# State space stage: squares of two chunks added on GpSimd, tail decays read off the decays, late decays moved beside the result, halves' bank moved

## The reference

```python
def ssd(x, A, B, C, chunk):
    ...
    Acs = jnp.cumsum(Ac, axis=-1)
    Lmat = jnp.exp(segsum(Ac))
    Y_diag = jnp.einsum('bclhn,bcshn,bhcls,bcshp->bclhp', Cc, Bc, Lmat, xc)
    decay_states = jnp.exp(Acs[..., -1:] - Acs)
    ...
    Y_off = jnp.einsum('bclhn,bchpn,bhcl->bclhp', Cc, states, jnp.exp(Acs))
    return (Y_diag + Y_off).reshape(b, l, h, p)

def mamba2_block(x, in_w, conv_w, conv_b, dt_bias, A_log, D, norm_w, out_w):
    ...
    zxbcdt = x @ in_w.T
    ...
    xBC = jax.nn.silu(y.transpose(0, 2, 1) + conv_b)
    dt = jax.nn.softplus(dt + dt_bias)
    ...
    y = ssd(xh * dt[..., None], A * dt, Bh, Ch, CHUNK)
    y = y + D[None, None, :, None] * xh
    ...
    y = rmsnorm(y * jax.nn.silu(z), norm_w)
    return y @ out_w.T
```

## Time and profile before

| | us |
|---|---|
| median of 3 runs | 2408.68 (2407.0 to 2409.1) |
| span of the profiled execution | 2405.4 |
| the state space stage in it | about 545 to 1022 |

### The profile page before, as it was taken

One profiled execution on the slowest core, in us unless ns is written; L12 is line 12 of the kernel. 1 busy time (PEld: TensorE's weight loads), 2 busy tenths in 40 slices (PEclk: granted clock), 3 DMA queues, 4 the chain that ended last, 5 costly groups with the idle time before them and its releaser, 6 DMA issues.

```text
span 2405.4 us, 39635 instructions
## 1 busy us (share of the span) xinstructions
PE 1979.7 (82%) x14320; PEld 1331.4 (55%) x14320; DVE 1549.6 (64%) x3583; ACT 1312.5 (55%) x2684; POOL 482.1 (20%) x539
## 2 busy tenths in 40 slices
PE   6999775988999999858874287999999898668796
PEld 4666562446777777633452154666666577424465
DVE  6877675766666666548849945766666456658543
ACT  4666533766777777525765235666666312337632
POOL 2112003204323323223004521001100001031033
PEclk9999986998999999968997588999999899869997
DMA  4000004400000000015301000000000100154012
GB/s 183 1 1 1 1 1 123 135 25 36 1 1 1 1 1 1 1 35 159 89 1 72 0 10 1 1 1 1 1 1 1 46 8 1 56 177 133 22 55 76
DMA packets 80162, 88.04 MB, mean 37 GB/s; under 512 B 6578, under 2 KB 70115, under 8 KB 78945
## 3 DMA queue, kind: packets, MB, share of 16 engines
q1 hardware_dynamic: 78625, 83.01, 11.1%
q0 software_dynamic: 1344, 2.49, 0.4%
HBM read 54.91 MB, written 30.70 MB: 36 GB/s over the span
## 4 chain that ended last, share of the span: by engine, by line
PE 56%; DVE 25%; ACT 8%; issue 7%; DMA 2%; POOL 1%; SPq 0%; DVEq 0%; ACTq 0%; POOLq 0%
PE bank L469 48%; DVE scratch L1226 3%; DVE w_keep L1927 2%; PE bank L653 1%; PE bank L2962 1%; PE bank L368 1%; DVE stats L245 1%; PE bank L693 1%; ACT w_early L3203 1%; DVE scratch L3101 1%; DVE scratch L721 1%; DVE w_early L2539 1%; DVE XN L3136 1%; PE bank L1195 1%; DVE scratch L3126 1%
## 5 line engine op out<-in xcount | busy, mean ns | idle before, releaser
L469 PE MATMUL bank<-scratch 64*128 64x256 bf16 (+5 forms) x3696 | 399.8, 320 | 81.9 <-DMA scratch<-parts 40.2
L469 PEld LDWEIGHTS bank<-scratch 64*128 64x128 bf16 (+3 forms) x3696 | 220.5, 123 | 231.7 <-issue 79.8
L1226 DVE TENSOR_REDUCE scratch<-bank 128x2 f32<-128x512 f32 x384 | 245.7, 686 | 97.5 <-PE bank L469 94.9
L469 PE MATMUL bank<-w_keep,scratch 128*128 128x128 f32 (+4 forms) x1760 | 247.1, 332 | 35.7 <-ACT scratch L806 20.8
L1312 ACT ACTIVATE w_keep<-bank 128x512 f32<-128x512 f32 x384 | 210.9, 597 | 70.0 <-PE bank L469 64.3
L469 PE MATMUL bank<-XNT,w_keep 128*128 128x256 f32 (+4 forms) x800 | 237.1, 435 | 7.2 <-POOL w_keep L2175 2.5
L469 PEld LDWEIGHTS bank<-w_keep,scratch 128*128 128x128 f32 (+3 forms) x1760 | 184.4, 185 | 97.2 <-issue 45.9
L3203 ACT ACTIVATE w_early<-bank,scratch 128x256 f32<-128x256 f32 x256 | 123.8, 564 | 130.9 <-DVE scratch L3105 130.9
L469 PEld LDWEIGHTS bank<-XNT,w_keep 128*128 128x128 f32 x800 | 148.7, 196 | 60.7 <-issue 29.4
L469 PE MATMUL bank<-w_early,scratch 64*128 64x256 f32 (+3 forms) x1152 | 164.9, 347 | 12.2 <-ACT w_early L3203 8.5
L469 PEld LDWEIGHTS bank<-w_early,scratch 64*128 64x128 f32 (+3 forms) x1152 | 119.7, 185 | 67.3 <-issue 41.3
(11 more groups left out here) (450 smaller groups left out, 3792.3 us busy)
## 6 DMA issues: line engine op xcount, KB each, us to landing
scratch<-parts SPq DMA_DIRECT2D x24, 1024.0 KB, 5.1
parts<-scratch SPq DMA_DIRECT2D x192, 96.0 KB, 2.4
parts<-scratch SPq DMA_DIRECT2D x96, 64.0 KB, 2.1
w_early<-pack_l3f SPq DMA_DIRECT2D x1, 5206.0 KB, 16.0
w_keep<-pack_l2f SPq DMA_DIRECT2D x1, 2124.0 KB, 13.7
w_early<-pack_mamba SPq DMA_DIRECT2D x1, 2120.0 KB, 19.0
w_keep<-pack_l2x SPq DMA_DIRECT2D x1, 2049.0 KB, 9.0
w_keep<-taps SPq DMA_DIRECT2D x4, 512.0 KB, 5.5
```

Source lines behind the costliest of these rows:

```text
L469: return pe.matmul(out, lhsT, rhs, start=start, stop=stop, skip_group_check=True)
L1226: dve.tensor_reduce(neg[:, :, h], self.k.bank[5 - g % 2][:, :].rearrange("p (t s) -> p t s", s=S), AXX, ALU.max, negate=True).then_inc(*s. ...
```

## The change

Four edits, all in `StateSpace`:

1. GpSimd gets a new instruction for each unit, `squares_pool(n-3)`, last in its iteration: it adds the squares of the two chunks in place. `mean_pe` then needs two matmuls where there were four, and waits for this sum (`s.pool.at("sq", ...)`) where it waited for ScalarE's squares.
2. The tail decays are no longer made by a matmul: ScalarE reads the last column of each head from the decays' bank in a 128x4 instruction of its own (in `decay_act`, t = 0), and `late_act` shrinks from 260 to 256 columns.
3. `late_pe` moves from the start of iteration u+1 into iteration u, behind the second part of the convolution and ahead of `result_pe`. Its use of bank 2 now comes after the output of unit n-5.
4. The `off` product moves from bank 2 to bank 0, which it shares with `raw` (`raw_bank`).

```diff
@@ -1690,7 +1690,13 @@
     def late_bank(self, n):
 
         s, there = self.k.s, lambda u: 0 <= u < UNITS
-        uses = [("late", n - 1, s.weighed, "late"), ("root", n - 5, s.lowered, "root"), ("out", n - 5, s.added, "final"), ("off", n - 2, s.normed, "off")]
+        uses = [("root", n - 5, s.lowered, "root"), ("out", n - 5, s.added, "final"), ("late", n, s.weighed, "late")]
+        return [x for x in uses if there(x[1])]
+
+    def raw_bank(self, n):
+
+        s, there = self.k.s, lambda u: 0 <= u < UNITS
+        uses = [("raw", n, s.stacked, "raw"), ("off", n - 2, s.normed, "off")]
         return [x for x in uses if there(x[1])]
 
     def small_bank(self, n):
@@ -1728,8 +1734,7 @@
     def raw_pe(self, pe, u):
         s, b, bank = self.k.s, u % B, self.k.bank[0]
         self.entered(pe, u)
-        if u >= 1:
-            pe.wait_ge(*s.stacked.at("raw", u - 1))
+        self.freed(pe, self.raw_bank, u, "raw")
         for j in range(2):
             m = mm(pe, bank[:, j * S:(j + 1) * S], self.weight(u, "xbc")[:, (INNER + j) * P:(INNER + j + 1) * P], self.k.XNT[:, b * S:(b + 1) * S])
         m.then_inc(*s.projected.up("raw", u))
@@ -1762,11 +1767,11 @@
         bank = self.k.bank[2]
         if u % PAIR == 0:
             pe.wait_ge(*s.formed.at("a", u))
-        self.freed(pe, self.late_bank, u + 1, "late")
+        self.freed(pe, self.late_bank, u, "late")
         for h in range(H_SSM):
             rows, cols = slice(HP * (h % 2), HP * (h % 2 + 1)), slice(h // 2 * P, (h // 2 + 1) * P)
-            mm(pe, bank[rows, cols], a3[:, 1, h:h + 1].to_broadcast([P, HP]), self.upto)
-        mm(pe, bank[:, S:S + H_SSM], self.k.w["after"], a3[:, 0, :]).then_inc(*s.scored.up("late", u))
+            m = mm(pe, bank[rows, cols], a3[:, 1, h:h + 1].to_broadcast([P, HP]), self.upto)
+        m.then_inc(*s.scored.up("late", u))
 
     def decay_pe(self, pe, u, t):
         s = self.k.s
@@ -1797,7 +1802,7 @@
         m.then_inc(*s.turned.up("x", u))
 
     def result_pe(self, pe, u):
-        s, out, late, xd, wt = self.k.s, self.k.bank[7], self.k.bank[2], self.xd[u % 2], self.by_head(self.wt[u % 2])
+        s, out, off, xd, wt = self.k.s, self.k.bank[7], self.k.bank[0], self.xd[u % 2], self.by_head(self.wt[u % 2])
         pe.wait_ge(*s.formed.at("xd", u))
         pe.wait_ge(*s.divided.at("weights", u))
         pe.wait_ge(*s.pool.at("weights", u))
@@ -1809,24 +1814,23 @@
                 m = mm(pe, out[rows, cols:cols + P], xd[:, t * D_INNER + h * HP:t * D_INNER + (h + 1) * HP], wt[:, t, h, :])
         m.then_inc(*s.summed.up("y", u))
         pe.wait_ge(*s.pool.at("xu", u))
-        self.freed(pe, self.late_bank, u + 2, "off")
+        self.freed(pe, self.raw_bank, u + 2, "off")
         for c in range(INNER):
-            m = mm(pe, late[:, c * P:(c + 1) * P], self.xu[u % 2][:, c * P:(c + 1) * P], self.gm[u % 2][:, 2 * P:3 * P])
+            m = mm(pe, off[:, c * P:(c + 1) * P], self.xu[u % 2][:, c * P:(c + 1) * P], self.gm[u % 2][:, 2 * P:3 * P])
         m.then_inc(*s.summed.up("off", u))
 
     def mean_pe(self, pe, u, j):
 
 
         s, bank = self.k.s, self.k.bank[3]
-        pe.wait_ge(*s.flip_s.at("sq", u + j))
+        pe.wait_ge(*s.pool.at("sq", u + j))
         if j or u + 3 < UNITS:
             self.freed(pe, self.small_bank, u + 4, "mean" if j else "g")
         else:
             self.freed(pe, self.small_bank, u + 4, "mean")
         for t in range(HALVES):
             at = MEAN_AT + j * HALVES + t
-            for c in range(INNER):
-                m = mm(pe, bank[:, at:at + 1], self.two(self.sq[(u + j) % 2])[:, c, t * P:(t + 1) * P], self.k.w["ones"][:, 0:1], c == 0, c == INNER - 1)
+            m = mm(pe, bank[:, at:at + 1], self.sq[(u + j) % 2][:, t * P:(t + 1) * P], self.k.w["ones"][:, 0:1])
         if j:
             m.then_inc(*s.rolled.up("mean", u))
 
@@ -1856,7 +1860,6 @@
             heads, prep, conv, proj = n - 2, n - 1, n, n - 5
             there = lambda u: 0 <= u < UNITS
             if there(prep):
-                self.late_pe(pe, prep)
                 self.decay_pe(pe, prep, 0)
             if n % PAIR == 0 and there(n - 4):
                 self.mean_pe(pe, n - 4, 0)
@@ -1876,6 +1879,8 @@
                 self.project_pe(pe, proj)
             if there(conv):
                 self.convolve_pe(pe, conv, 1)
+            if there(conv):
+                self.late_pe(pe, conv)
             if there(heads):
                 self.result_pe(pe, heads)
             if there(prep):
@@ -1967,7 +1972,7 @@
                                          in1=self.two(bank[:, :])[:, c, :], op0=ALU.mult, op1=ALU.add)
         o.then_inc(*s.flip_v.up("skip", u))
         dve.wait_ge(*s.summed.at("off", u))
-        dve.tensor_tensor(self.off[u % 2], self.k.bank[2][:, 0:S], self.late[u % 2][:, 0:S], ALU.mult).then_inc(*s.normed.up("off", u))
+        dve.tensor_tensor(self.off[u % 2], self.k.bank[0][:, 0:S], self.late[u % 2][:, 0:S], ALU.mult).then_inc(*s.normed.up("off", u))
 
     def mean_dve(self, dve, u):
         s, n, r = self.k.s, PAIR * HALVES, self.roots(u)
@@ -2050,14 +2055,18 @@
         act.wait_ge(*s.scored.at("late", u))
         if u >= 2:
             act.wait_ge(*s.normed.at("off", u - 2))
-            act.wait_ge(*s.pool.at("xu", u - 2))
-        act.activation(self.late[u % 2], self.k.bank[2][:, 0:S + H_SSM], ACT.Exp).then_inc(*s.weighed.up("late", u))
+        act.activation(self.late[u % 2][:, 0:S], self.k.bank[2][:, 0:S], ACT.Exp).then_inc(*s.weighed.up("late", u))
 
     def decay_act(self, act, u, t):
         s = self.k.s
         act.wait_ge(*s.scored.at("decay", u, t))
         if u >= 2:
             act.wait_ge(*s.summed.at("y", u - 2))
+        if t == 0:
+            if u >= 2:
+                act.wait_ge(*s.pool.at("xu", u - 2))
+            ends = columns_of(self.k.bank[5][:, :], P - 1, (P, H_SSM))
+            act.activation(self.late[u % 2][:, S:S + H_SSM], ends, ACT.Exp)
         act.activation(self.by_head(self.wt[u % 2])[:, t, :, :], self.k.bank[5 + t][:, :].rearrange("p (h s) -> p h s", s=P),
                        ACT.Exp).then_inc(*s.weighed.up("decay", u, t))
 
@@ -2148,7 +2157,7 @@
     def middle_pool(self, pool, u):
         s, heads = self.k.s, lambda ap: ap.rearrange("p (h w) -> p h w", w=HP)
         pool.wait_ge(*s.formed.at("xd", u))
-        pool.wait_ge(*s.weighed.at("late", u))
+        pool.wait_ge(*s.weighed.at("decay", u, 0))
         if u >= 2:
             pool.wait_ge(*s.summed.at("off", u - 2))
         pool.tensor_tensor(heads(self.xu[u % 2]), heads(self.xd[u % 2][:, 0:D_INNER]), self.late[u % 2][:, S:S + H_SSM].unsqueeze(2).to_broadcast([P, H_SSM, HP]),
@@ -2161,6 +2170,12 @@
         pool.tensor_tensor(second, second, self.two(self.off[u % 2]), ALU.add).then_inc(*s.pool.up("sum", u))
         pool.wait_ge(*s.pool.at("sum", u))
         pool.tensor_tensor(z, y, z, ALU.mult).then_inc(*s.pool.up("gated", u))
+
+    def squares_pool(self, pool, u):
+
+        s, sq = self.k.s, self.sq[u % 2]
+        pool.wait_ge(*s.flip_s.at("sq", u))
+        pool.tensor_tensor(sq[:, 0:S], sq[:, 0:S], sq[:, S:2 * S], ALU.add).then_inc(*s.pool.up("sq", u))
 
     def presets_pool(self, pool):
         k, s = self.k, self.k.s
@@ -2198,6 +2213,8 @@
                 self.gated_pool(pool, heads)
             if there(prep):
                 self.middle_pool(pool, prep)
+            if there(n - 3):
+                self.squares_pool(pool, n - 3)
             if n in (2, 3, 4):
                 self.taps_pool(pool, n - 1)
```

## The result

The changed kernel took **2521.7 us** (median; 2512.8 to 2525.6) against 2408.1 for the kernel before: a ratio of 1.046, with a 95% interval of 1.0444 to 1.0476. That is 113.6 us more where 82 was forecast, and 1.7 us above the upper end of the range. The span of the profiled execution is 2520.0 against 2405.4, 114.6 more.

The account below looks back on a forecast made before the run. The prediction took a 28.82 us cycle per two units, through TensorE, VectorE's softplus and ScalarE, as the bound. Waits 3.64 plus clock 1.5 made 5.14 a pair, 82 over 16 pairs: 2405.4 + 82 + 3.3 = 2491, range 2455 to 2520.

Parts of the forecast that it names:

- Direction and mechanism: State space stage: TensorE's mean waits twice a pair for GpSimd's squares, making the kernel slower (chance 0.93).
- The two new waits: TensorE ahead of the means: 2.0 us in the odd half, 3.05 in the even; ahead of late about 1.7.
- The price of the squares: GpSimd's new instruction behind `xu`: 0.70 us for 256 columns, with ends 0.61 and 0.90.
- What is hidden: ScalarE's new 128x4 instruction: hidden behind the late exponentials, taken as 0 rather than 0.21 us.
- The waits' price without the clock: Waits with TensorE at 2.4 GHz: 3.64 us a pair, 58 over 16 pairs; as a rival 2467, chance 0.20.
- The clock: TensorE falls to 1.2 GHz after the 3.05 us gap in each pair, 1.5 us more; none after the 2.0 gap.
- clock also falls after the shorter gap: Rival: also a fall after the 2.0 gap or the wait ahead of late, 1.5 us more a pair, 2515; chance 0.18.
- savings in the second half of the pair vanish in the wait for ScalarE: Second half of the pair: TensorE already waits for ScalarE there, so matmuls removed count only in the first half.
- free: Bank edit: moving `off` to bank 0 costs nothing apart from late's wait, since `raw` was read long before.

Follow-up runs that it names:

- E2: Kernel before with edit 1 alone (squares added on GpSimd last in its iteration, mean halved): 2493.7 us, 1.0399.
- E1: Changed kernel without edit 1 (mean keeps four matmuls and waits for ScalarE's squares; edits 2 to 4 stay): 2402.22 us, 1.0016 against the kernel before.
- E3: Changed kernel with GpSimd's squares right behind its weights, ahead of the gated product: 2423.23 us, 1.0105 against the kernel before.
- E7: Kernel before with edits 2 and 4 alone (tail decays read from the decays' bank, off product in bank 0): 2412.66 us, 1.0055.
- E4: Changed kernel with idle matmuls in TensorE's gaps ahead of both means (3 and 5 of 256 columns): 2455.46 us, 1.0242 against the kernel before.
- E6: E5 with GpSimd adding only the pair's first unit's squares, the second mean keeping four matmuls: 2400.09 us, 1.0007 against the kernel before.
- E5: E3 with late's matmuls back at the start of the next iteration: 2416.11 us, 1.0077 against the kernel before.
- E8: E3 with three idle matmuls of 256 columns in TensorE's wait ahead of late: 2409.1 us, 1.005 against the kernel before.

## Why the prediction was right in kind and short in size

- **Direction and mechanism: right.** TensorE waits for L2178 twice a pair, and edit 1 alone costs 94.6 (E2), the other three alone 3 (E1). That they cost more on top of edit 1 (some 16 to 19) fits the clock's fall after the gap of 2.02, but no run isolates it.
- **The two new waits: right.** Forecast 2.0 and 3.05, measured 2.02 and 2.98; ahead of late 1.7, measured 1.69. The places in the cycle, by the pair without a fall in its first half: first mean 12.88 (forecast 13.15), even root 15.15 (15.36), late 22.41 (22.62), second mean 28.87 (29.30), odd root 33.69 with one fall (32.46 and 1.5 make 33.96). Most of what the means are early by lies ahead of `y`: late delays it by 0.49 and 0.46 (700.51 to 701.00, 716.52 to 716.98), not by 0.59 each time, and in the first half starts 0.07 sooner than `y` did. The rest is in small steps: `y` to VectorE's sums took 1.09 and 1.11 instead of 1.15, and the squares start 0.57 after `xu` instead of 0.61.
- **The price of the squares: right.** 719 ns in the mean, against 0.70 taken from the instruction's neighbours in the trace. The estimate of 0.56, by division of the figure in the Trainium skill's GPSIMD Engine Reference (section 3.1, Elementwise — side-by-side cycle accounting), was 0.16 too low. Its rule (section 4.1, Engine selection), that elementwise work on two inputs goes to VectorE, no run here tests: none adds the squares there. What the runs show is that the instruction's place in GpSimd's list made these waits, since with the same instruction early in the list (E3) they are gone.
- **What is hidden: right.** ScalarE's new reading of the last columns costs nothing that shows: in E7, which has it, the half of the pair that ends in the wait for ScalarE takes 14.98, before 14.99.
- **The waits' price without the clock: right.** Forecast 58 (3.64 a pair, 16 pairs), measured 56.3 in E4. The cycle was 3.19 more there, not 3.64, which makes 51 for 16 pairs. The other 5 must lie at the stage's ends, where the clock is still low in E4 (7 by the estimate above). So this term came out near partly by luck: it has 0.45 a pair too much for the waits, and 56.3 holds some of the clock's price.
- **The clock: the step that failed.** I took "1.5 more" for one fall a pair and "none in the likeliest case" for the gap of 2.0. Measured are 3.6 a pair (35.61 less 32.01). Two sizes were off in that term. The gap of 2.0 lost the clock in 9 of 12 pairs, where the two of eight gaps of 1.88 had let me leave it out. And behind the long gap a fall cost 1.7 (4.82 less 3.13) or 3.0 (6.14 less 3.13), since low stretches came in two lengths (3.4, and 6.8 in 5 of 21), where I had one piece of 3.0 us for 1.5. The trace had both: the piece is part of a stretch of 3.4 (608.5 to 611.9), and behind the gap of 2.99 ahead of 1454.38, the one of the earlier trace rows, the stretch is 6.8 long (from 1455.0). Over the whole kernel the clock has 113.6 less 56.3, 57 of the 114 us or somewhat more, where the sum had 24. That the two numbers come from different chips matters little: the kernel before differs by 0.4% between them.
- **The rival "clock also falls after the shorter gap", 2515,** was thus what happened in most pairs, but with 1.5 for a fall it too stayed 7 short. The range ended on it with 6 for the squares and nothing for a longer fall; that bound of the clock's price was missing from it.
- **The rest of the loss.** The 12 cycles make 12 x (35.61 less 28.82) = 81.5 of the 114.6 of the span; the other four pairs and the ends have 33, some 8 each. There TensorE waits 3.63 and 3.40 for L2178 (ahead of 1108.94 and 1120.13), and the clock is low for 6.8 and 20.5 us (from 1109.3 and 1119.6).
- **Edits 2 and 4 and the root's wait.** I said that savings in the second half of the pair vanish in the wait for ScalarE, and called the move of `off` to bank 0 free. E7 shows that this is too kind: the saved matmul and the wait that `off` no longer has lengthen it (1.36 to 2.29) and turn a gain of 0.2 into a loss of 1.5 in each pair where the clock falls. In the changed kernel this didn't happen, as late, moved, takes the wait for `final_dve` itself. I had priced the wait ahead of late and had not asked this of the wait that was there.

What stays open is why the same wait of 2.02, 2.29 or 2.81 is followed by a fall in one pair and not in the next. In E6 every second pair has one, in E5 and E7 three of four; the runs don't say what decides it.

## What to carry to other kernels

Before moving work from a busy engine to an idle one, ask when the idle engine's turn comes in its own list, not how much time it has to spare: here an addition of 0.72 us, last of four in a row, cost some 50 us in waits and about as much by the clock behind them. Then treat each wait of TensorE that your change makes or lengthens as a price with two parts, the wait and the clock behind it, and take the second from rows of the clock after gaps of that size, with both the share of gaps that lose it and the longest low stretch. Where a wait can't be avoided, a few idle matmuls that end before it does kept the clock here; with them a saving ahead of the wait is worth having, and without them it can be a loss. That holds for a saved matmul as for an earlier wait that an edit takes away: both bring TensorE to the next wait sooner.

## What the runs showed of the hardware that I had not expected

- In the middle of this stage, waits of TensorE of 1.3 to 1.8 us never lost the clock (E1: 1.31 and 1.68, E8: 1.76 in every pair, clock 1.00 from 620 to 1000); 2.02 lost it in 9 of 12 pairs, 2.16 in 10 of 12 (E3), 2.29 in three of four (E7) or every second (E6), 2.81 in three of four (E5), 2.98 in 12 of 12. The length of the one gap doesn't decide alone: at the stage's start the kernel before has a wait of 1.17 (ahead of 607.24) and the clock low from 608.5. In the rows above the granted clock reads 1.00 in the gap and 0.50 behind it; in a gap of 4.25 of E2 it is 0.50 already inside it (from 720.7, with the mean at 722.50).
- In the middle of the stage a low stretch lasted 3.4 us or 6.8 (in the changed kernel 5 of 21), at its end up to 20.5. In E3, E5, E6 and E7 all of those in the middle of the stage were 3.4.
- A multiplication of 16 columns on VectorE (L1604) took 0.65 us where it overlapped GpSimd's sum of 256 columns, and 0.17 at the same place of the kernel before. A second one (L1602) took 0.97 beside GpSimd's 512 columns in the kernel before, and each ended within 0.03 of GpSimd's instruction. Not every small instruction is held up: the reciprocal of 16 columns ahead of L1602 (L1600, one input, 743.51) took 0.25 beside the same 512 columns. No run takes GpSimd's instruction away from L1602, so that the overlap does it rests on these three.
